# First token tiles and weights of a conditional mixture-of-LoRA layer: another order and other pieces on two DMA queues

## The chip, the cores and the metric

The kernel runs on one NeuronCore of a Trainium2 chip. The metric is the device time of one execution in microseconds (us). A core has TensorE (PE, matrix products into PSUM), VectorE (DVE), ScalarE (ACT), GpSimd (POOL) and SyncE (SP), each with its own instruction stream, and 16 DMA engines that all of them share. Here SyncE, ScalarE and GpSimd issue transfers. Engines wait for each other through semaphores.

## The reference

There are 8 sequences of 256 tokens with 1024 features in float32. Each sequence picks one of 8 weight matrices by its number. The result goes through a layer with a base matrix and a router that mixes two of eight rank-16 adapters, and is added to x:

```
w = weight[adapter_ids]
xc = jnp.einsum('bsi,boi->bso', x, w)
logits = xc @ W_router.T                       # softmax, top 2 of 8, renormalised -> combine
h = jnp.einsum('nd,erd->ner', xc, A_stack) * combine[..., None]
lora_out = jnp.einsum('ner,eor->no', h, B_stack) * 2.0
out = x + xc @ W_base.T + b_base + lora_out
```

## The kernel before

Every float32 operand of a product is split in two: a high part, which ScalarE makes with a cast, and a low part, which VectorE makes by subtracting the high one. The names are `x_hl` for tokens and `wc_hl` for weights. A product of high and low parts is then summed from several TensorE products of the fast float32 form.

The work runs in 2 groups of 4 sequences. For each sequence s, `cond` makes 8 output tiles t of the first einsum. A tile takes 8 steps k over the features: 8 wide products (line 801: high weights by high and low tokens, 512 columns) and then 8 narrow ones (line 805: low weights by high tokens, 256 columns). Router, adapters and the base matrix follow, the last in `second` with seven block products. Results leave through `out_sb`.

Raw float32 data comes in through `raw`, six slots of 512 KB (128 partitions of 4 KB). SyncE issues nearly all of these loads in one fixed order, `LOADS`, and before each waits until the slot's last user has been split (`wait_free`). A half of a sequence's tokens is one slot, ("x", s, half), with 4 of the 8 k. The weights of one output tile are one slot, ("w", s, t), with all 8 k. SyncE first reads the expert numbers from memory (line 362), because the address of a weight tile depends on them; it does so ahead of its first issue.

The first tiles are treated apart, by tables at lines 56 to 65. `START` gives the slots: X0 and X1 are the two token halves of sequence 0, W0 and W1 its first two weight tiles. `ACT_MOVES` and `SP_MOVES` list the pieces (tile, from k, to k) that ScalarE and SyncE issue, in order. A row of a piece is one partition's part of it. `HI_PIECES` and `LO_PIECES` list the pieces in which ScalarE casts (line 490) and VectorE subtracts (line 666), in order; each piece waits for the transfer or the cast that it needs. `START_STEPS` lists the steps (t, from k, to k) of `first_cond` on TensorE: all wide products of the step, then all its narrow ones. A wide product of step k waits for the high part of the weights at k and for the low part of the tokens at k; a narrow one waits for the low weights. From weights 2 on, ScalarE and VectorE take whole tiles (lines 472 and 536). Before its first real product TensorE does 26 products on zeroes (line 913).

Of the kernel before, what the change touches and what calls it, by code (L numbers as in the profile page):

```python
# [53 lines left out]


STARTS = 4
START = [("x", 0, 0), ("x", 0, 1), ("w", 0, 0), ("w", 0, 1), ("w", 0, 2), ("w", 0, 3)]
X0, X1, W0, W1 = range(STARTS)
ACT_MOVES = [(X0, 0, 4), (X1, 0, 4)]
SP_MOVES = [(W0, 0, 4), (W0, 4, 8), (W1, 0, 4), (W1, 4, 8)]  # L60
HI_PIECES = [(X0, 0, 2), (X0, 2, 4), (X1, 0, 2), (X1, 2, 4), (W0, 0, 2), (W0, 2, 4), (W0, 4, 8), (W1, 0, 4),
             (W1, 4, 8)]
LO_PIECES = [(X0, 0, 2), (X0, 2, 4), (X1, 0, 2), (X1, 2, 4), (W0, 0, 4), (W0, 4, 8), (W1, 0, 4), (W1, 4, 8)]

START_STEPS = [(0, 0, 8), (1, 0, 4), (1, 4, 8)]
WARM, WARM_N = 26, 2 * P

RESIDENT = {(0, 5): [("a", 0, 0)], (2, 5): [("b", 0, 0)]}
# [58 lines left out]
def split_order():  # L127

    order = START[STARTS:]
    for g in range(GROUPS):  # L130
# [23 lines left out]
def load_order():  # L154

    out, n = [], 0
    for g in range(GROUPS):
        ring = list(START) if g == 0 else []
        for s in range(GSEQS * g, GSEQS * (g + 1)):
# [19 lines left out]
def piece_count(pieces, i, k):  # L179

    return next(n + 1 for n, (j, a, b) in enumerate(pieces) if j == i and a <= k < b)


def tile_steps(i):
    return KT if START[i][0] == "w" else HT

# [19 lines left out]
def build(nc, x, ids, w_cond, w_base, w_router, lora_a, lora_b, bias, consts, out):  # L206
    with ExitStack() as ctx:
# [6 lines left out]
        def sem(name):  # L214
            return ctx.enter_context(nc.semaphore(name))
# [44 lines left out]
        raw_in = [sem(f"raw_in{i}") for i in range(RAW)]  # L260
        start_in = {(i, b): sem(f"start_in{i}_{b}") for i, a, b in ACT_MOVES + SP_MOVES if b < tile_steps(i)}
        warm_clear = sem("warm_clear")
# [49 lines left out]
        def split_dst(key, hl):  # L312
            kind, i, j = key
            if kind == "w":
                return wc_hl[:, slot_of(i, j), hl]
            if kind == "x":
                return x_hl[:, i % 2, HT * j:HT * (j + 1), hl, :]
            if kind == "S":
                return wc_hl[:, pair_of(i, j[0]) + j[1], hl]
            if kind == "T":  # L320
                return half(t_buffer(j[0]), j[1])[:, :, hl]
            if kind == "a":
                return a_hl[:, hl]
            return b_hl[:, hl, 0:KT] if kind == "b" else b_hl[:, hl, KT:]

        def split_src(key):
            kind, i, j = key
            if kind == "T":
                return half(t_plain(j[0]), j[1])
            if kind == "S":  # L330
                slot = S_FROM[j[0]] + j[1]
            else:
                slot = LANDED[("b", 0, 0) if kind == "bd" else key][0]
            v = raw[:, slot].rearrange("p (k n) -> p k n", n=TOK if kind == "x" else P)
            return v[:, 0:HT] if kind == "bd" else v

        def piece(v, i, a, b):

            n = v.shape[1] // tile_steps(i)
            return v[:, a * n:b * n]  # L340

        def piece_in(i, b):
            return raw_in[i] if b == tile_steps(i) else start_in[i, b]

        def move_piece(issuer, i, a, b, src):
            issuer.dma_start(piece(raw[:, i], i, a, b), piece(src, i, a, b)).then_inc(piece_in(i, b), 16)  # L346

        def moved(i, k):

            return piece_in(i, next(b for j, a, b in ACT_MOVES + SP_MOVES if j == i and a <= k < b))  # L350

        @block.sync
        def _(sp):
            ids_of = {}

            def source(key):
                kind, i, j = key
                if kind == "x":
                    return x[i, j]
                if kind == "w":  # L360
                    if i not in ids_of:
                        ids_of[i] = nc.sync.value_load(ids[0:1, i:i + 1], min_val=0, max_val=w_cond.shape[0] - 1)  # L362
                    return w_cond[bass.ds(ids_of[i], 1), j, :, :].rearrange("a p n -> (a p) n")
                if kind in ("a", "b"):
                    return lora_a if kind == "a" else lora_b
                oh, ih = next(q for name, _, q in QUARTERS if name == kind)
                return w_base[oh, ih, :, j, :]

            def wait_free(key):
# [6 lines left out]
                elif kind in ("A11", "A12", "A22", "A22b"):  # L376
                    j = {"A11": P7, "A12": P2, "A22": P3, "A22b": P4}[kind]
                    sp.wait_ge(lo_done, SPLIT["S", g, (j, h)])
                elif key in START[:STARTS]:
                    i = START.index(key)  # L380
                    sp.wait_ge(start_lo, piece_count(LO_PIECES, i, tile_steps(i) - 1))
                else:
                    sp.wait_ge(lo_done, SPLIT[("bd", 0, 0) if kind == "b" else key])

            in_slot = {}
            for i, a, b in SP_MOVES:
                move_piece(nc.sync, i, a, b, source(START[i]))
            for n, (key, slot) in enumerate(LOADS):
# [60 lines left out]
        def _(act):  # L449
# [35 lines left out]

            for i, a, b in ACT_MOVES:
                move_piece(nc.scalar, i, a, b, x[START[i][1], START[i][2]])
            for i, a, b in HI_PIECES:
                act.wait_ge(moved(i, b - 1), 16)
# [41 lines left out]
        def _(dve):  # L531
# [131 lines left out]

            for i, a, b in LO_PIECES:
                dve.wait_ge(start_hi, piece_count(HI_PIECES, i, b - 1))
                nc.vector.tensor_tensor(piece(split_dst(START[i], LO), i, a, b), piece(split_src(START[i]), i, a, b),
# [116 lines left out]
        def _(pe):  # L783
# [16 lines left out]
            def wide(ps, s, t, k):  # L800
                nc.tensor.matmul(ps[:], wc_hl[:, slot_of(s, t), HI, k], x_hl[:, s % 2, k].rearrange("p h n -> p (h n)"),  # L801
                                 start=(k == 0), stop=False)

            def narrow(ps, s, t, k):
                return nc.tensor.matmul(ps[:, TOK:], wc_hl[:, slot_of(s, t), LO, k], x_hl[:, s % 2, k, HI],  # L805
                                        start=False, stop=(k == KT - 1))

            def first_cond():

                for t, a, b in START_STEPS:  # L810
                    w, ps = (W0, W1)[t], bank_x[t]
                    for k in range(a, b):
                        pe.wait_ge(start_hi, piece_count(HI_PIECES, w, k))
                        pe.wait_ge(start_lo, piece_count(LO_PIECES, X0 if k < HT else X1, k % HT))
                        wide(ps, 0, t, k)
                    for k in range(a, b):
                        pe.wait_ge(start_lo, piece_count(LO_PIECES, w, k))
                        mm = narrow(ps, 0, t, k)
# [159 lines left out]
```

## Time and profile before

| | us |
|---|---|
| median of 3 runs | 396.82 |
| lowest and highest of them | 396.25, 397.05 |
| the profiled execution's own time | 396.74 |
| its span in the trace | 394.9 |
| TensorE busy in it | 389.9 (99%) |
| VectorE, ScalarE busy | 305.3, 183.7 |

The busy share tells how near an engine is to being the bound; the waits tell where it is not fed; the chain of work tells what released each step. DMA issues show in the rows of SPq and ACTq at the time of their issue, not of their transfer. Where a row of ScalarE says "idle before <-DMA", the transfer had landed at the row's start.

### The profile page before, as it was taken

The numbers are of one execution on the slowest core, as the hardware profiler recorded it, in microseconds if no ns is written. First come the engines' busy times: TensorE is split into PE (matmuls) and PEld (weight loads), VectorE is DVE, ScalarE is ACT, GpSimd is POOL, SyncE is SP. The second block draws the span as 40 slices with busy tenths as digits, with TensorE's granted clock in tenths as the row PEclk, the third lists the DMA queues.
The fourth block names the chain that finished last, engine by engine and source line by source line (L and its number), as shares of the span: only waits on it lengthen the run. The fifth ranks groups of instructions, "written<-read, shape, count | busy, mean of one in ns | idle before, by whom it ended". The sixth has DMA issues, their size and how long they took to land.

```text
span 394.9 us, 5677 instructions
## 1 busy us (share of the span) xinstructions
PE 389.9 (99%) x2174; PEld 332.1 (84%) x2174; DVE 305.3 (77%) x441; ACT 183.7 (47%) x282; POOL 40.1 (10%) x68
## 2 busy tenths in 40 slices
PE   8999999999999999999999999999999999999996
PEld 7888888888888888888888888888888888888885
DVE  4797967779699999984457786878867999999311
ACT  5777734748632434332146676356656224441000
POOL 0101100110000130021172000000000001301110
PEclk9999999999999999999999999999999999999999
DMA  7998782768430135586669877356073102462222
GB/s 259 391 341 310 282 299 80 272 217 309 146 106 0 54 115 173 192 289 218 218 222 369 337 240 240 108 168 244 15 266 122 41 1 80 162 185 80 82 80 80
DMA packets 21083, 72.96 MB, mean 185 GB/s; under 512 B 2816, under 2 KB 2832, under 8 KB 21056
## 3 DMA queue, kind: packets, MB, share of 16 engines
q1 hardware_dynamic: 15840, 55.58, 40.6%
q0 software_dynamic: 4928, 15.97, 11.3%
q10 hardware_dynamic: 288, 1.05, 0.7%
q8 instruction: 17, 0.28, 0.3%
q14 instruction: 10, 0.08, 0.1%
HBM read 64.20 MB, written 8.39 MB: 184 GB/s over the span
## 4 chain that ended last, share of the span: by engine, by line
PE 97%; DMA 1%; SPq 1%; DVE 0%; ACT 0%; issue 0%
PE bank_x L801 30%; PE bank_x L805 15%; PE bank_y L786 9%; PE bank_y L787 9%; PE bank_y L788 9%; PE bank_x L787 8%; PE bank_x L788 8%; PE bank_x L786 8%; PE bank_y L845 2%; DMA raw<-w_cond 1%; SPq L362 1%; PE bank_y L865 0%; DVE out_sb L587 0%; ACT wc_hl L490 0%; SPq L346 0%
## 5 line engine op out<-in xcount | busy, mean ns | idle before, releaser
L801 PE MATMUL bank_x<-x_hl,wc_hl 128*128 128x512 f32 x512 | 128.7, 392 | 0.6 <-ACT wc_hl L490 0.6
L536 DVE TENSOR_TENSOR wc_hl<-raw,wc_hl 128x1024 fp32r<-128x1024 f32 x90 | 108.4, 1221 | 19.0 <-ACT wc_hl L472 18.9
L472 ACT CAST wc_hl<-raw 128x1024 fp32r<-128x1024 f32 x90 | 93.4, 1050 | 55.6 <-DVE raw L540 23.1
L801 PEld LDWEIGHTS bank_x<-x_hl,wc_hl 128*128 128x128 f32 x512 | 92.2, 189 | 17.8 <-ACT wc_hl L490 1.2
L805 PEld LDWEIGHTS bank_x<-x_hl,wc_hl 128*128 128x128 f32 x512 | 70.0, 190 | 5.1
L805 PE MATMUL bank_x<-x_hl,wc_hl 128*128 128x256 f32 x512 | 71.5, 282 | 0.0
L424 POOL DMA_DIRECT2D out<-out_sb x28 | 15.3, 545 | 249.8 <-DVE out_sb L587 228.5
L504 ACT COPY xc_low<-bank_x 128x256 f32<-128x256 f32 x64 | 23.6, 369 | 32.6 <-PE bank_x L805 32.6
L786 PE MATMUL bank_x<-x_hl,wc_hl 128*128 128x512 f32 x96 | 37.3, 389 | 0.0
L787 PE MATMUL bank_x<-x_hl,wc_hl 128*128 128x512 f32 x96 | 37.3, 389 | 0.0
L788 PE MATMUL bank_x<-x_hl,wc_hl 128*128 128x512 f32 x96 | 37.3, 389 | 0.0
L687 DVE TENSOR_TENSOR xp<-bank_x,xc_low 128x256 f32<-128x256 f32 x64 | 26.9, 421 | 13.1 <-ACT xc_low L504 12.4
L509 ACT CAST xc_hl<-xp 128x256 fp32r<-128x256 f32 x64 | 26.0, 406 | 22.8 <-DVE xp L687 22.6
L579 DVE SCALAR_TENSOR_TENSOR out_sb<-bank_x,bias_sb,out_sb 128x512 f32<-128x512 f32 x32 | 23.6, 746 | 15.8 <-PE bank_x L788 15.1
L692 DVE TENSOR_TENSOR xc_hl<-xp,xc_hl 128x256 fp32r<-128x256 f32 x64 | 26.9, 420 | 7.5 <-ACT xc_hl L509 7.5
L587 DVE TENSOR_TENSOR out_sb<-bank_y,out_sb 128x512 f32<-128x512 f32 x24 | 16.4, 689 | 18.4 <-PE bank_y L788 17.6
L418 POOL DMA_DIRECT2D out_sb<-x x32 | 22.7, 714 | 73.9 <-PE bank_x L805 73.6
L786 PE MATMUL bank_y<-xc_hl,wc_hl 128*128 128x512 f32 x64 | 24.9, 389 | 0.0
L787 PE MATMUL bank_y<-xc_hl,wc_hl 128*128 128x512 f32 x64 | 24.9, 389 | 0.0
L788 PE MATMUL bank_y<-xc_hl,wc_hl 128*128 128x512 f32 x64 | 24.9, 389 | 0.0
L472 ACT CAST x_hl<-xp 128x1024 fp32r<-128x1024 f32 x16 | 16.6, 1052 | 15.1 <-DVE xp L540 14.7
L786 PEld LDWEIGHTS bank_x<-x_hl,wc_hl 128*128 128x128 f32 x96 | 18.0, 188 | 3.8
(91 smaller groups left out, 481.6 us busy)
## 6 DMA issues: line engine op xcount, KB each, us to landing
raw<-w_cond SPq DMA_DIRECT2D x62, 512.0 KB, 4.6
raw<-w_base SPq DMA_DIRECT2D x24, 512.0 KB, 5.2
out_sb<-x POOLq DMA_DIRECT2D x32, 256.0 KB, 5.1
raw<-x SPq DMA_DIRECT2D x14, 512.0 KB, 4.6
out<-out_sb POOLq DMA_DIRECT2D x28, 256.0 KB, 2.3
raw<-x ACTq DMA_DIRECT2D x2, 512.0 KB, 3.6
raw<-w_cond SPq DMA_DIRECT2D x4, 256.0 KB, 3.6
out<-out_sb SPq DMA_DIRECT2D x4, 256.0 KB, 2.0
```

Of the source, the lines that this page charges most:

```text
L472: nc.scalar.copy(split_dst(key, HI), split_src(key)).then_inc(hi_done, 1)
L504: nc.scalar.copy(xc_low[:, t % 2], bank_x[t % HT][:, TOK:]).then_inc(low_copied, 1)
L509: nc.scalar.copy(xc_hl[:, t, HI, s % 2 * TOK:(s % 2 + 1) * TOK], xp[:, s // 2 % 2, t, s % 2 * TOK:(s % 2 + 1) * TOK]).then_inc(xc_hi, 1)
L536: nc.vector.tensor_tensor(split_dst(key, LO), split_src(key), split_dst(key, HI).bitcast(F32), ALU.subtract).then_inc(lo_done, 1)
L579: nc.vector.scalar_tensor_tensor(out_sb[:, o], bank_x[m][:], bias_sb[:, i:i + 1], out_sb[:, o], ALU.add, ALU.add).then_inc(pass_done, 1)
L687: nc.vector.tensor_tensor(xc, bank_x[t % HT][:, 0:TOK], xc_low[:, t % 2], ALU.add) \
L692: nc.vector.tensor_tensor(xc_hl[:, t, LO, s % 2 * TOK:(s % 2 + 1) * TOK], xc, xc_hl[:, t, HI, s % 2 * TOK:(s % 2 + 1) * TOK].bitcast(F32), ...
L786: nc.tensor.matmul(ps, w_hi, v_hi, start=start, stop=False, skip_group_check=resumed)
L787: nc.tensor.matmul(ps, w_hi, v_lo, start=False, stop=False, skip_group_check=resumed)
L788: return nc.tensor.matmul(ps, w_lo, v_hi, start=False, stop=stop, skip_group_check=resumed)
L801: nc.tensor.matmul(ps[:], wc_hl[:, slot_of(s, t), HI, k], x_hl[:, s % 2, k].rearrange("p h n -> p (h n)"), start=(k == 0), stop=False)
L805: return nc.tensor.matmul(ps[:, TOK:], wc_hl[:, slot_of(s, t), LO, k], x_hl[:, s % 2, k, HI], start=False, stop=(k == KT - 1))
```

## The change

Only the tables of the start change. ScalarE's queue moves X0 alone, in two pieces of two k each, whose rows are 2 KB. X1 goes to SyncE's queue as one piece, behind the first half of W0 and ahead of its second half. ScalarE casts and VectorE subtracts in the new order of arrival, and the second half of W0 is cast in two pieces of two k. The first output tile is computed in two steps of four k, each with its wide and its narrow products, instead of one step of eight. The slots of X1 and W0 change places.

```diff
-START = [("x", 0, 0), ("x", 0, 1), ("w", 0, 0), ("w", 0, 1), ("w", 0, 2), ("w", 0, 3)]
-X0, X1, W0, W1 = range(STARTS)
-ACT_MOVES = [(X0, 0, 4), (X1, 0, 4)]
-SP_MOVES = [(W0, 0, 4), (W0, 4, 8), (W1, 0, 4), (W1, 4, 8)]
-HI_PIECES = [(X0, 0, 2), (X0, 2, 4), (X1, 0, 2), (X1, 2, 4), (W0, 0, 2), (W0, 2, 4), (W0, 4, 8), (W1, 0, 4),
-             (W1, 4, 8)]
-LO_PIECES = [(X0, 0, 2), (X0, 2, 4), (X1, 0, 2), (X1, 2, 4), (W0, 0, 4), (W0, 4, 8), (W1, 0, 4), (W1, 4, 8)]
-
-START_STEPS = [(0, 0, 8), (1, 0, 4), (1, 4, 8)]
+START = [("x", 0, 0), ("w", 0, 0), ("x", 0, 1), ("w", 0, 1), ("w", 0, 2), ("w", 0, 3)]
+X0, W0, X1, W1 = range(STARTS)
+ACT_MOVES = [(X0, 0, 2), (X0, 2, 4)]
+SP_MOVES = [(W0, 0, 4), (X1, 0, 4), (W0, 4, 8), (W1, 0, 4), (W1, 4, 8)]
+HI_PIECES = [(X0, 0, 2), (X0, 2, 4), (W0, 0, 2), (W0, 2, 4), (X1, 0, 2), (X1, 2, 4), (W0, 4, 6), (W0, 6, 8),
+             (W1, 0, 4), (W1, 4, 8)]
+LO_PIECES = [(X0, 0, 2), (X0, 2, 4), (W0, 0, 4), (X1, 0, 2), (X1, 2, 4), (W0, 4, 8), (W1, 0, 4), (W1, 4, 8)]
+
+START_STEPS = [(0, 0, 4), (0, 4, 8), (1, 0, 4), (1, 4, 8)]
```

What it moves on the engines. On SyncE, at the head of its stream, behind the reads of the expert numbers (the first weight piece, then the second):

```order
 L346 ISA
 L346 DMA raw<-w_cond 128x512
+L346 DMA raw<-x 128x1024
 L346 ISA
 L346 DMA raw<-w_cond 128x512
```

The transfer of X1 now stands between the two halves of W0; all that follows is the same, one transfer further back.

On ScalarE, from its transfers to the first whole weight tiles, before:

```order
1 L346 DMA raw<-x 128x1024 x2
2 L490 ACT_TABLE_LOAD
3 L490 CAST x_hl<-raw 128x2x256 x4
4 L490 CAST wc_hl<-raw 128x256 x2
5 L490 CAST wc_hl<-raw 128x512 x3
6 L472 CAST wc_hl<-raw 128x1024 x2
```

and after:

```order
1 L346 DMA raw<-x 128x512 x2
2 L490 ACT_TABLE_LOAD
3 L490 CAST x_hl<-raw 128x2x256 x2
4 L490 CAST wc_hl<-raw 128x256 x2
5 L490 CAST x_hl<-raw 128x2x256 x2
6 L490 CAST wc_hl<-raw 128x256 x2
7 L490 CAST wc_hl<-raw 128x512 x2
8 L472 CAST wc_hl<-raw 128x1024 x2
```

The two casts of X1 moved behind those of W0's first half, and W0's second half is two casts of two k.

On TensorE, from the warm-up to the third output tile, before:

```order
1 L913 MATMUL bank_y<-gate_rows 128x256 x26
2 L801 MATMUL bank_x<-x_hl,wc_hl 128x512 x8
3 L805 MATMUL bank_x<-x_hl,wc_hl 128x256 x8
4 L801 MATMUL bank_x<-x_hl,wc_hl 128x512 x4
5 L805 MATMUL bank_x<-x_hl,wc_hl 128x256 x4
6 L801 MATMUL bank_x<-x_hl,wc_hl 128x512 x4
```

and after:

```order
1 L913 MATMUL bank_y<-gate_rows 128x256 x26
2 L801 MATMUL bank_x<-x_hl,wc_hl 128x512 x4
3 L805 MATMUL bank_x<-x_hl,wc_hl 128x256 x4
4 L801 MATMUL bank_x<-x_hl,wc_hl 128x512 x4
5 L805 MATMUL bank_x<-x_hl,wc_hl 128x256 x4
6 L801 MATMUL bank_x<-x_hl,wc_hl 128x512 x4
```

Four narrow products of the first tile moved ahead of its last four wide ones.

## Rows read from the trace of the kernel before

**Rows 1.** The page's first part: busy time, share of the span, instructions.

```profile
PE 389.9 (99%) x2174; PEld 332.1 (84%) x2174; DVE 305.3 (77%) x441; ACT 183.7 (47%) x282; POOL 40.1 (10%) x68
```

**Rows 2.** TensorE's waits behind the warm-up: total us, times, longest.

```profile
PE bank_x L801 <- ACT wc_hl L490: 0.6, 2, 0.3
```

**Rows 3.** Chain of work, first 20 us: start us, us, what.

```profile
0.73 0.96 SPq L362
...
1.73 1.33 SPq L362
...
4.14 3.43 DMA raw<-w_cond
...
8.26 1.19 PE bank_x L801 x4
9.45 0.94 PE bank_x L805 x8
10.39 0.93 PE bank_x L801 x4
...
13.20 1.84 PE bank_x L801 x8
...
15.99 1.84 PE bank_x L801 x8
```

**Rows 4.** ScalarE in order of time: start us, us, operation, idle before it.

```profile
0.74 0.86 ACTq L346 DMA_DIRECT2D raw<-x  x2
...
4.01 2.36 ACT L490 CAST x_hl<-raw 128x512 fp32r<-128x512 f32 x4 [1.09 <-DMA raw<-x]
6.31 0.71 ACT L490 CAST wc_hl<-raw 128x256 fp32r<-128x256 f32 x2
7.59 0.62 ACT L490 CAST wc_hl<-raw 128x512 fp32r<-128x512 f32 x1 [0.56 <-DMA raw<-w_cond]
8.44 0.62 ACT L490 CAST wc_hl<-raw 128x512 fp32r<-128x512 f32 x1 [0.23 <-DMA raw<-w_cond]
10.43 0.62 ACT L490 CAST wc_hl<-raw 128x512 fp32r<-128x512 f32 x1 [1.38 <-DMA raw<-w_cond]
11.72 1.05 ACT L472 CAST wc_hl<-raw 128x1024 fp32r<-128x1024 f32 x1 [0.67 <-DMA raw<-w_cond]
13.02 1.06 ACT L472 CAST wc_hl<-raw 128x1024 fp32r<-128x1024 f32 x1 [0.25 <-DMA raw<-w_cond]
```

**Rows 5.** TensorE in order of time, from the warm-up to the first tile.

```profile
1.20 5.29 PE L913 MATMUL bank_y<-gate_rows 128*128 128x256 f32 x26 [1.20 <-DVE gate_rows L532]
...
6.77 1.19 PE L801 MATMUL bank_x<-x_hl,wc_hl 128*128 128x512 f32 x4 [0.29 <-ACT wc_hl L490]
8.26 1.19 PE L801 MATMUL bank_x<-x_hl,wc_hl 128*128 128x512 f32 x4 [0.30 <-ACT wc_hl L490]
```

**Rows 6.** SyncE's first issues in order of time.

```profile
3.56 2.00 SPq L346 DMA_DIRECT2D raw<-w_cond  x4
```

**Rows 7.** Stretches: busy us and instructions by engine, clock, DMA share, GB/s.

```profile
0.00:1.50 1.50, 0.30 (x1) 0.30 (x2) 0.27 (x1) 0.00 (x0) 0.40 (x5) 1.00 0.00 0
...
5.50:6.00 0.50, 0.50 (x6) 0.50 (x6) 0.50 (x2) 0.50 (x2) 0.00 (x0) 1.00 1.09 356
...
1.20:5.00 3.80, 3.80 (x18) 3.80 (x19) 0.34 (x1) 2.27 (x3) 0.00 (x0) 1.00 0.79 286
2.50:3.70 1.20, 1.20 (x7) 1.20 (x7) 0.00 (x0) 0.42 (x1) 0.00 (x0) 1.00 1.05 423
5.60:10.40 4.80, 4.21 (x25) 3.32 (x24) 3.55 (x6) 2.67 (x6) 0.00 (x0) 1.00 0.91 295
10.40:13.00 2.60, 2.60 (x16) 2.24 (x16) 0.89 (x2) 1.67 (x2) 0.00 (x0) 1.00 1.01 406
```

**Rows 8.** Groups of VectorE and ScalarE at the start: count, busy us, mean ns.

```profile
L666 DVE TENSOR_TENSOR x_hl<-raw,x_hl 128x512 fp32r<-128x512 f32 x4 | 2.5, 688 | 3.5 <-ACT x_hl L490 3.5
...
L490 ACT CAST wc_hl<-raw 128x256 fp32r<-128x256 f32 x2 | 0.7, 403 | 0.0
```

## The prediction

> **What bounds the kernel now.** I read the busy totals first: TensorE is busy 389.9 of 394.9 us [rows 1]. Then its waits: after its warm-up it waits twice, 0.6 us in all, both times for a ScalarE cast of weights [rows 2], and both waits lie before 8.3 us [rows 5]. From there to the last product nothing is late for TensorE, so whatever delays its stream in the first 15 us moves the end by the same amount, and whatever it saves there is at most those two gaps, 0.29 + 0.30 us. The third view is the chain of work at the start [rows 3]. The reader is to see in it that the chain goes over SyncE: 0.96 and 1.33 us of reading the expert numbers, then the issues, then 3.43 us until the second half of the first weights has landed, then a cast [rows 4] and the four 512-column products at 8.26. The fourth view is ScalarE's order of work [rows 4]: each cast there that stands behind an idle stretch ended by a DMA starts when that DMA has landed, so the view is a ladder of landings. In megabytes of SyncE's queue, which begins with nothing before it: the first 0.25 MB (first half of W0) by 6.31 at the latest (ScalarE was busy until then), 0.5 MB (second half of W0) 7.59, 0.75 MB (first half of W1) 8.44, 1.0 MB (second half of W1) 10.43, 1.5 MB (weights 2) 11.72, 2.0 MB (weights 3) 13.02. These rungs carry the forecast.
>
> **The first tokens on ScalarE's queue.** ScalarE issues at 0.74 [rows 4], while SyncE's first issue is at 3.56 [rows 6], behind the reads of the expert numbers. Before, ScalarE's two issues (1 MB) fill that time. Afterwards its queue holds only X0, 0.5 MB. X0 whole was castable at 4.01 [rows 4]; as two pieces the first should be castable about 0.6 us earlier (256 KB at the 423 GB/s of that stretch [rows 7]), the second at about 4.0 to 4.2, since rows of half the length may cost a little. Nothing on the path wants it: its last low half is done by 4.2 + 0.62 + 0.69 = 5.5 [rows 4, 8], and the first weights come at about 6. With X1 gone from this queue there is nothing for the 16 DMA engines to move from about 4.0 until SyncE's stream starts, one microsecond after its first issue (ScalarE's first issue at 0.74 had moved nothing by 1.5 [rows 4, 7]), so at about 4.6. The time is lost, not shifted.
>
> **The first half step.** W0's first half stays first on SyncE's queue. The casts of X1 no longer stand ahead of it on ScalarE (two of the four that ran to 6.37 [rows 4]), so its first cast may start at its landing. TensorE's warm-up runs to 6.49 and the first real product was at 6.77 [rows 5], so the gain here is between 0 and 0.28 us. TensorE then does four wide products and, new, the four narrow ones of the same k, and is through with them by about 8.1. That takes four narrow products, half of the 0.94 us of eight [rows 3], off what stands behind W0's second half. Neither gain is on the path by itself: the second half step waits for X1 and for W0's second half, wherever these are.
>
> **The second half step.** W0's second half was at 0.5 MB of SyncE's queue and is now at 1.0 MB, behind X1. Call its landing L. The cast of its first two k is 0.40 [rows 8] instead of 0.62, and a handover is about 0.04 (7.59 + 0.62 to 8.26), so TensorE goes on at L + 0.44. Then come four wide and four narrow products, 1.19 + 0.47 = 1.66. Before, this point was 8.26 + 1.19 + 0.94 = 10.39 [rows 3]. The shift of TensorE's stream is therefore L + 0.44 + 1.66 - 10.39 = **L - 8.29**. X1 is a second bound on the same start, because ScalarE casts it ahead of these k: it is at 0.75 MB, 8.44 by the ladder, ScalarE's two casts of it end 1.24 later at 9.68, and with 0.44 for W0's first two k the start is not before 10.12. Counted in starts, the shift is (start + 1.66 - 10.39), here +1.4.
> - Upper end of L: the rung as it stands, 10.43, a shift of +2.1. It contains the largest step of the ladder, 1.99 us for 256 KB, where the others are 0.65 to 1.28.
> - Evened out, the ladder goes from 6.31 to 13.02 in seven steps of 256 KB, 0.96 each, so L = 6.31 + 2.88 = 9.19, a shift of +0.9; X1 is then at 8.23, which by the bound above gives a start at 9.91 and +1.2.
> - Lower end: the stream at 406 GB/s from 4.6, as after 10.4 us [rows 7], not at the 295 of 5.6 to 10.4. Then X1 lands near 6.8, ScalarE's two casts end at 8.0, two k of W0 follow, TensorE goes on at 8.5: a shift of -0.2.
>
> **Behind it.** Every later piece also stands 0.5 MB further back. W1's first half, at 1.25 MB, lands at 11.07 by the ladder (half way from 10.43 to 11.72); with a cast of 0.62 it allows a start at 11.74 where before it was 10.39: a shift of at least 1.35. Evened out it is 10.15 and at least 0.4. Weights 2, at 2.0 MB, land at 13.02, are cast by 14.07, and the third product started at 13.20 [rows 3]: at least +0.9 in both readings. So the term that the landings of W0's second half give is backed by the two that follow it, and I take **+1.4 us**: the evened readings give 0.9 to 1.2, the rungs as they stand 1.35, 1.4 and 2.1, and only one of these asks for more. After weights 2 the stream brings a tile in 1.3 us and TensorE uses one in 2.79 (13.20 to 15.99), so nothing further is added. The load of weights 5 goes into the slot that now held W0, not X1, and its issue waits for W0's last low half, about 11 us; SyncE is held there, with weights 6 behind it. Its turn in the stream comes at about 15 and TensorE wants it at 13.20 + 3 x 2.79 = 21.6: cost nothing. VectorE and ScalarE do the same work plus one split cast (two of 0.40 for one of 0.62; its 0.18 is in the start that I reckon with).
>
> **Sum.** The profiled run was 396.74 us (span 394.9 and 1.8 around it), 0.08 under the median of 396.82. Plus 1.4 that is 398.1 against itself, and 398.2 against the median.
>
> **A rule against the trace.** The rows show SyncE's first issue 2.8 us after ScalarE's. The Trainium skill, page "DMA: Bandwidth & Descriptors", section "Issuing engines are not separate DMA queues", says that issuing from several engines only saves the sequencer's time to issue. By it the move of X1 would cost one issue, about 0.4 us, and the sum would be 397.2. The trace agrees that the engines are shared, but here one of the queues starts late, and that the rule leaves out.
>
> **Rivals.** (1) *The slow stretch is not one of bytes.* From 5.6 to 10.4 the engines moved 295 GB/s, after that 406 [rows 7]. If that was peculiar to the half-length weight pieces, and X1's full-length rows come at 406, X1 lands at 6.8 to 7.8, W0's second half at 7.6 to 9.1 and the shift is -0.2 to +0.8, in the middle +0.4: 397.2. For it: the x tiles moved at 423 on ScalarE's queue [rows 7]. Against it: the stretch also took in full-length weights. It decides where X1 lands before 7.8 and L is below 9.1. (2) *TensorE's clock falls in the new gap.* TensorE would now idle from about 8.1 to 9.6 or later, where its longest gap was 0.30. In the warm-up 18 products of 256 columns took 3.80 us [rows 7], 211 ns each, which is 1.2 GHz, where a narrow one later takes 0.94 / 8 = 118 ns; the slower pace held from 1.2 to about 5.5, where six such products take half a microsecond [rows 7]. The same again would cost 4.3 x (1 - 118 / 211) = 1.9 us on top: 400.1. For it: the gap is five times any other. Against it: TensorE has then worked for 7 us with few pauses. The page "TensorE: Matmul & The Clock Gate" of the Trainium skill (section "Part 1: The HAM clock gate") says that an idle engine falls back to half rate. The trace shows no fall after its two short gaps, and its column of the granted clock reads 1.00 even in the warm-up, so here it is the pace that tells. (3) *Faster.* The only time to win is the two gaps, 0.58 us, less than 0.2% of the whole; it needs L below 7.7.
>
> **How the numbers follow.** A measurement of this kernel can tell about 0.2%, 0.8 us, from no change. Forecast, slower without a fall of the clock: 0.60, itself 397.7 to 399.1. Rival 1, within 0.2%: 0.24. Rival 2, slower: 0.13. Faster by more than 0.2%, by something not named here: 0.03. So slower 0.73, same 0.24, faster 0.03. The range must leave out no more than two in ten: from 397.0 (most of rival 1) to 399.8 (L as late as 11.4, the ladder's rung and one step more), leaving rival 2 outside.
>
> **What would show it.** Right: ScalarE's first weight cast at or before 6.3; a wait of TensorE behind eight products, 1.4 to 2.7 us long, ended by a cast of W0 or by the low half of X1; the DMA share near zero between 4.0 and 4.6; the third product at 14.1 to 15.3 instead of 13.20; all later rows moved by the same amount. Wrong: the second half step starting before 9.3, a stretch from 4.6 to 8 at over 380 GB/s, products at 211 ns after the gap, or an end that moves by another amount than the third product does.

## The result and the profile after

The changed kernel takes 397.56 us (median of 22 runs, 396.89 to 399.77), the kernel before 396.70 (22 runs, 396.12 to 397.57). The ratio is 1.0024, 95% interval 1.0017 to 1.003: slower by 0.7 to 1.2 us, on the side and in the range that were forecast, and less than the +1.4 of the sum. It also lies just below the 397.7 to 399.1 that the prediction gave its main case. The profiled run took 397.39 us with a span of 395.6, against 396.74 and 394.9, so 0.7 us more.

ScalarE in order of time, the rows that answer to [rows 4] (start us, us, operation, idle before it and what ended it):

```profile
0.74 0.86 ACTq L346 DMA_DIRECT2D raw<-x  x2
...
3.42 1.22 ACT L490 CAST x_hl<-raw 128x512 fp32r<-128x512 f32 x2 [0.50 <-DMA raw<-x]
5.72 0.71 ACT L490 CAST wc_hl<-raw 128x256 fp32r<-128x256 f32 x2 [1.08 <-DMA raw<-w_cond]
7.73 1.14 ACT L490 CAST x_hl<-raw 128x512 fp32r<-128x512 f32 x2 [1.30 <-DMA raw<-x]
8.77 1.75 ACT L490 CAST wc_hl<-raw 128x256 fp32r<-128x256 f32 x4
11.34 1.05 ACT L472 CAST wc_hl<-raw 128x1024 fp32r<-128x1024 f32 x1 [0.81 <-DMA raw<-w_cond]
```

X1 was castable (landed, with ScalarE waiting for it) at 7.73; before, the casts of both x tiles were over by 6.37 [rows 4]. Behind it ScalarE does not wait again until 11.34: W0's second half was in before its casts began at 8.77. So of the two bounds that the prediction had for the second half step it was X1 with its casts, not W0's second half.

TensorE in the same view, which answers to [rows 5]:

```profile
1.20 5.16 PE L913 MATMUL bank_y<-gate_rows 128*128 128x256 f32 x26 [1.20 <-DVE gate_rows L532]
6.19 1.18 PE L801 MATMUL bank_x<-x_hl,wc_hl 128*128 128x512 f32 x4
7.21 0.74 PE L805 MATMUL bank_x<-x_hl,wc_hl 128*128 128x256 f32 x4
9.22 1.29 PE L801 MATMUL bank_x<-x_hl,wc_hl 128*128 128x512 f32 x4 [1.28 <-ACT wc_hl L490]
10.35 0.72 PE L805 MATMUL bank_x<-x_hl,wc_hl 128*128 128x256 f32 x4
```

The first half step starts at 6.19 instead of 6.77 and is done at 7.9. Then the new gap of 1.28 us opens. The chain of work, against [rows 3]:

```profile
1.60 0.66 SPq L362
...
3.20 4.51 DMA raw<-x
7.70 0.02 issue
7.73 1.14 ACT x_hl L490 x2
8.87 0.31 ACT wc_hl L490
9.18 0.04 issue
9.22 1.29 PE bank_x L801 x4
10.51 0.55 PE bank_x L805 x4
11.06 0.93 PE bank_x L801 x4
...
13.87 1.86 PE bank_x L801 x8
```

It goes over X1's transfer, 4.51 us from issue to landing, and no longer over W0's second half. The third tile's products start at 13.87 where it was 13.20. The second output tile starts at 11.06 where it was 10.39, so these 0.67 us are complete there, and they are the 0.7 by which the span grew: nothing was added or given back behind. The first row of this chain holds what the prediction did not have. The second of the two loads that read the expert numbers took 0.66 us, where it took 1.33 before [rows 3], and SyncE's first issue was at 2.76 instead of 3.56 [rows 6].

### The profile page after: what moved, and what is told of

Read it like the earlier page. It is cut to its first block, busy times and chain, and to the rows that moved or that the text cites. A ratio compares the mean times of both kernels' runs of the same rounds, so it can differ in the third digit from the quotient of the medians.

```text
span 395.6 us, 5679 instructions
## 1 busy us (share of the span) xinstructions
PE 389.9 (99%) x2174; PEld 331.9 (84%) x2174; DVE 305.5 (77%) x441; ACT 183.9 (46%) x283; POOL 40.1 (10%) x68
## 4 chain that ended last, share of the span: by engine, by line
PE 97%; DMA 1%; SPq 1%; ACT 0%; DVE 0%; issue 0%
PE bank_x L801 30%; PE bank_x L805 15%; PE bank_y L786 9%; PE bank_y L787 9%; PE bank_y L788 9%; PE bank_x L787 8%; PE bank_x L788 8%; PE bank_x L786 8%; PE bank_y L845 2%; DMA raw<-x 1%; SPq L362 0%; ACT x_hl L490 0%; PE bank_y L865 0%; DVE out_sb L587 0%; SPq L346 0%
## 5 line engine op out<-in xcount | busy, mean ns | idle before, releaser
L424 POOL DMA_DIRECT2D out<-out_sb x28 | 15.3, 545 | 249.8 <-DVE out_sb L587 228.5
```

## The experiments

Column two is the difference of the medians of the kernel and of the kernel before, run on the same chip; column three is the ratio that the comparison gave, with its interval; the two differ a little where the runs of a kernel spread. The last column counts the runs whose mean granted clock of TensorE was 0.996 or lower. Where only some runs of a kernel have it, these are its longest ones: with X0 in pieces and the steps alone, three runs took 397.80 to 398.22 us and three 399.72 to 400.26. There the median mixes two things, a late operand and a slower TensorE.

| kernel | us over before | ratio (95% interval) | clock 0.996 or lower |
|---|---|---|---|
| the change | +0.86 | 1.0024 (1.0017 to 1.003) | 1 of 22 |
| steps only | -0.13 | 0.9992 (0.9983 to 1.0001) | 0 of 12 |
| X1 back on ScalarE's queue | +0.78 | 1.0017 (1.0007 to 1.0027) | 1 of 12 |
| X1 alone moved | +4.40 | 1.0095 (1.0074 to 1.0115) | 4 of 4 |
| X1 alone moved, 52 warm-up products | +2.21 | 1.0059 (1.0046 to 1.0072) | 0 of 5 |
| X1 first on SyncE's queue | +1.13 | 1.0025 (1.0015 to 1.0035) | 2 of 11 |
| the change, X0 whole | +1.02 | 1.0026 (1.0016 to 1.0036) | 0 of 8 |
| the same, X1 back | +0.06 | 1.0001 (0.9993 to 1.001) | 0 of 11 |
| steps only, X0 in pieces | +2.12 | 1.0059 (1.004 to 1.0078) | 3 of 6 |
| the same, SyncE held | +0.72 | 1.0019 (1.001 to 1.0027) | 1 of 12 |
| the change, numbers not read | +2.45 | 1.0065 (1.0052 to 1.0078) | 3 of 5 |
| before, numbers not read | +3.49 | 1.009 (1.0077 to 1.0103) | 5 of 5 |
| steps only, W0 and W1 whole | +0.14 | 1.0006 (0.9998 to 1.0015) | 0 of 11 |

### First four: which part costs

Steps only:

```diff
 HI_PIECES = [(X0, 0, 2), (X0, 2, 4), (X1, 0, 2), (X1, 2, 4), (W0, 0, 2), (W0, 2, 4),
-             (W0, 4, 8), (W1, 0, 4), (W1, 4, 8)]
+             (W0, 4, 6), (W0, 6, 8), (W1, 0, 4), (W1, 4, 8)]
-START_STEPS = [(0, 0, 8), (1, 0, 4), (1, 4, 8)]
+START_STEPS = [(0, 0, 4), (0, 4, 8), (1, 0, 4), (1, 4, 8)]
```

> The kernel before with the other part of the change: both x tiles on ScalarE's queue as before, only the first output tile in two steps of four k and W0's second half cast in two pieces. Theory A: the four early narrow products fill the wait ahead of W0's second half; -0.2 to -0.45 us. Theory B: +0.3 to +0.9 us.

It measured -0.13 us, with an interval that just reaches no change. The steps are not what costs (this part of theory B falls here; the other part, W0 cast ahead of X1, is taken up by the last four runs). TensorE ran from 7.14 on without a pause, so the early narrow products do fill the second gap of [rows 5]. W0's first half landed at 6.68 in that profile, later than 6.31, which took part of the gain there; the interval, -0.7 to 0.0 us, does not tell the measurement from the -0.2 to -0.45 that were expected.

X1 back on ScalarE's queue:

```diff
-ACT_MOVES = [(X0, 0, 2), (X0, 2, 4)]
-SP_MOVES = [(W0, 0, 4), (X1, 0, 4), (W0, 4, 8), (W1, 0, 4), (W1, 4, 8)]
+ACT_MOVES = [(X0, 0, 2), (X0, 2, 4), (X1, 0, 4)]
+SP_MOVES = [(W0, 0, 4), (W0, 4, 8), (W1, 0, 4), (W1, 4, 8)]
```

> The changed kernel with X1 issued by ScalarE again, behind X0's two pieces; SyncE's queue is then W0, W0, W1, W1 as before, and all piece and step orders stay those of the change. Theory A (the cost is that X1's bytes are moved after SyncE's late start instead of before it, so W0's second half and all behind it come 0.5 MB later): X1 lands near 5, W0's second half near 7.6, the second half step starts at 8.3 to 8.8, and the time is -0.4 to +0.1 us against the kernel before. Theory B (the cost is in the new pieces and steps: more and smaller casts, W0 cast ahead of X1): it stays +0.5 to +0.9 us.

It measured +0.78 us. Theory A, as written, missed: putting X1 back gives almost nothing back, and the time is the one that theory B had expected. ScalarE's order shows another wait in its place, which theory B does not have:

```profile
4.75 0.62 ACT L490 CAST x_hl<-raw 128x512 fp32r<-128x512 f32 x1 [0.71 <-DMA raw<-x]
7.35 0.71 ACT L490 CAST wc_hl<-raw 128x256 fp32r<-128x256 f32 x2 [1.99 <-DMA raw<-w_cond]
7.97 1.14 ACT L490 CAST x_hl<-raw 128x512 fp32r<-128x512 f32 x2
```

SyncE issued W0's first half at 2.80, 0.76 us earlier than before, and yet it landed at 7.35 and not by 6.31. X0's last piece was castable at 4.75 and not at 4.0. From SyncE's start on both queues were moving at once.

X1 alone moved, casts and steps as before:

```diff
-ACT_MOVES = [(X0, 0, 4), (X1, 0, 4)]
-SP_MOVES = [(W0, 0, 4), (W0, 4, 8), (W1, 0, 4), (W1, 4, 8)]
+ACT_MOVES = [(X0, 0, 4)]
+SP_MOVES = [(W0, 0, 4), (X1, 0, 4), (W0, 4, 8), (W1, 0, 4), (W1, 4, 8)]
```

> The kernel before with one part of the change: X1 goes to SyncE's queue between W0's halves, while X0 stays one piece and the casts and steps keep the old order (X1 cast ahead of W0, one step of eight k). Theory A: all first products now wait for X1, near 7.7 to 8.4, and for two casts of it and one of W0, so TensorE starts at 9.4 to 10.1 with eight wide and eight narrow products ahead; +1.4 to +2.2 us against before, more than the whole change costs, because the half step does not hide any of it. Theory B: within 0.3 us of before.

It measured +4.4 us, twice what was expected. The first product came at 9.67, inside the 9.4 to 10.1 of theory A. The rest is mostly TensorE's pace. The first eight wide products, where 1.84 is usual [rows 3], and the stretches around them (the third number from the right is the granted clock):

```profile
9.67 3.78 PE L801 MATMUL bank_x<-x_hl,wc_hl 128*128 128x512 f32 x8 [3.26 <-ACT wc_hl L490]
```

```profile
6.40:9.60 3.20, 0.01 (x1) 0.00 (x0) 0.78 (x2) 1.43 (x4) 0.00 (x0) 0.88 0.97 321
9.60:13.40 3.80, 3.73 (x9) 2.97 (x10) 3.15 (x6) 2.96 (x7) 0.00 (x0) 0.50 1.02 403
13.40:16.00 2.60, 2.60 (x13) 2.42 (x12) 2.55 (x3) 1.82 (x3) 0.00 (x0) 0.57 1.01 400
```

The granted clock read 0.50, its level of 1.2 GHz, when work came again after a gap of 3.26 us, and it stayed there over the eight products.

X1 first on SyncE's queue, ahead of the read of the numbers:

```diff
-SP_MOVES = [(W0, 0, 4), (X1, 0, 4), (W0, 4, 8), (W1, 0, 4), (W1, 4, 8)]
+SP_MOVES = [(X1, 0, 4), (W0, 0, 4), (W0, 4, 8), (W1, 0, 4), (W1, 4, 8)]
```

> The changed kernel with X1 still on SyncE's queue but issued ahead of the reads of the expert numbers, at about 0.75. Theory A: X1 moves in the time that the change left empty and lands near 5; the reads of the numbers and so the weights start 0.4 us later; second half step at 8.6 to 9.2, 0.0 to +0.5 us against before, better than the change. Theory C (it is the queue: 0.5 MB more on SyncE's queue ahead of the weights costs the same wherever it is issued): +0.8 us or more.

It measured +1.13 us, outside what theory A gave and in the range of theory C. But it does not decide for theory C, since the weights started late. Both loads of the read became longer, in the view of line 362 (durations in ns, least, middle, greatest; start):

```profile
L362 SPq TENSOR_LOAD <-ids_ptr x1: 1540/1540/1540, 1.2 to 1.2; - x1
L362 SPq TENSOR_LOAD <-ids x1: 1517/1517/1517, 2.7 to 2.7; - x1
```

They took 0.96 and 1.33 us before [rows 3]. SyncE's first weight issue came at 4.75 instead of 3.56. Right behind the issue of X1 on its own queue the read of the numbers took longer. In the profiled run TensorE waited 2.02 us and its clock fell here too: four wide products took 2.08 us, at a granted clock of 0.50 from 8.00 to 10.10. That run is one of the two long ones of eleven (398.87 us); the other nine took 397.77 to 398.25 us at a mean clock of 0.999 or more, so the +1.13 us of the median holds no such fall.

### Second four: the rows of X0, the clock, the read

The change with X0 whole:

```diff
-ACT_MOVES = [(X0, 0, 2), (X0, 2, 4)]
+ACT_MOVES = [(X0, 0, 4)]
```

> The changed kernel with one part undone: X0 is one transfer of 4 KB rows again; all else stays changed. In five profiles so far SyncE's read of the expert numbers took 1.33 to 1.52 us beside whole x tiles and 0.66 to 0.67 beside X0's 2 KB pieces. Theory A2 (X1's place costs the forecast 1.4 us, and the shorter read gives 0.7 back): the read is at 1.3 to 1.5 again, SyncE's first issue at 3.5 to 3.6 instead of 2.8, and the time is +0.5 to +0.9 us above the changed kernel, +1.3 to +1.8 above before; the gap of TensorE grows and its pace may drop in some runs. Rival (the read's time is chance, or X0's pieces cost as much as they give): within 0.3 us of the changed kernel.

It measured +1.02 us against before, and by the ratios the same as the change (1.0026 and 1.0024). The first half of theory A2 held: the read's second load took 1.41 us and the first issue was at 3.53. The second half fell, and the rival (within 0.3 us of the changed kernel) held: the earlier issue in the changed kernel was worth little, since X1 landed at 7.93 here and at 7.73 there. DMA stretches of this run, the last number GB/s:

```profile
3.70:4.60 0.90, 0.90 (x6) 0.90 (x6) 0.00 (x0) 0.64 (x2) 0.00 (x0) 1.00 0.13 11
4.60:5.60 1.00, 1.00 (x6) 1.00 (x6) 0.99 (x2) 0.50 (x1) 0.00 (x0) 1.00 0.73 248
5.60:7.60 2.00, 1.86 (x12) 1.39 (x10) 0.95 (x2) 0.71 (x2) 0.00 (x0) 1.00 0.93 330
```

This is the empty stretch that the prediction named: 11 GB/s where the kernel before has 405 in the same 0.9 us.

Steps only, X0 in pieces:

```diff
-ACT_MOVES = [(X0, 0, 4), (X1, 0, 4)]
+ACT_MOVES = [(X0, 0, 2), (X0, 2, 4), (X1, 0, 4)]
```

> The steps-only kernel with X0 in two pieces of 2 KB rows, X1 behind it on ScalarE's queue; the casts keep the old order, X1 ahead of W0. It is the changed kernel with X1 back on ScalarE's queue and cast where it used to be. Theory A2 (the place of X1, with the cast order that goes with it, is what costs): first issue of SyncE at 2.8, X1 near 5.3, second half step at 8.4 or before; -0.5 to -0.1 us against before, so 1.0 to 1.4 us better than the change. Theory D (three issues and short rows on ScalarE's queue delay W0's first half to 7.35, as in the run with X1 put back): first product at 7.8, +0.1 to +0.6 us against before.

It measured +2.12 us, worse than either theory had it. Three of the six runs have the lower clock; the three without it took 397.93 us in the middle, +1.1, so about half of the median's loss goes with the clock, as far as the mean clocks tell; no trace of the three longer runs is at hand. The profiled run (397.93 us) is one without it. The read was short again (0.64 us) and SyncE issued at 2.76. X1, which everything waits for in this order of casts, was late:

```profile
6.84 1.14 ACT L490 CAST x_hl<-raw 128x512 fp32r<-128x512 f32 x2 [2.04 <-DMA raw<-x]
```

The chain in this profile is X1's transfer, 5.18 us from 1.64 on, and the first product came at 8.34. Weights that started 0.8 us earlier went through the same engines as X1. TensorE's gap was 1.71 us in this profile.

X1 alone moved, with 52 products on zeroes instead of 26:

```diff
-WARM, WARM_N = 26, 2 * P
+WARM, WARM_N = 52, 2 * P
```

> The kernel with X1 alone moved to SyncE's queue (measured at +4.4 us), with 52 products on zeroes instead of 26, which fill most of TensorE's gap of 3.26 us. If part of those 4.4 us is TensorE's slower pace after the gap (eight wide products took 3.78 us there, 1.84 elsewhere), the eight wide products take about 1.9 us and the time falls by 1.5 to 2.2 us, to +2.2 to +2.9 us against before. If all of it is the late arrival of X1, the time stays.

It measured +2.21 us, 2.2 us less for 26 more products that compute nothing, at the edge of what was expected. The granted clock reads 1.00 from 6.40 to 11.50, and the eight wide products took 1.92 us in the chain. The first real product came at 9.32 instead of 9.67, so up to 0.35 us of the gain may be a start that came earlier in that run. The clock's share of the +4.4 is then about 2 us, an estimate from these two kernels, and the rest is X1's late arrival.

The change without the read of the numbers for the first sequence:

```diff
+                if kind == "w" and i == 0:
+                    return w_cond[3, j]
                 if kind == "w":
                     if i not in ids_of:
```

> The changed kernel with the first sequence's weights taken at a fixed expert, 3, so that SyncE issues without the read of the numbers (the first sequence's result is then another; the numbers are read ahead of the second sequence's first weights). Theory A2 (late start of SyncE's queue is what makes X1's move dear): SyncE's first issue at 0.75, W0, X1 and W0's second half landed by about 6, no gap behind the first half step, real products from 6.2 without a pause: -1.3 to -0.9 us against before. Rival (X1 ahead of W0's second half costs wherever the queue starts, in casts and order): a wait of over 0.5 us stays behind the first half step.

It measured +2.45 us where theory A2 expected -1.3 to -0.9. Three of the five runs have the lower clock; the two without it, the profiled one among them, took 398.39 and 398.54 us, +1.5 and +1.7. SyncE issued at 0.76, 2.0 us earlier than in the change, and the kernel became slower. X0's second piece was castable at 7.51 instead of about 4.0, the first product came at 8.49. That refuted the idea behind my first theory, that the only harm lies in a queue's late start. The rival missed too: behind the first half step TensorE did not wait at all, since everything was late together.

### Last four: which bytes come first

The change with X0 whole and X1 back on ScalarE's queue:

```diff
-ACT_MOVES = [(X0, 0, 4)]
-SP_MOVES = [(W0, 0, 4), (X1, 0, 4), (W0, 4, 8), (W1, 0, 4), (W1, 4, 8)]
+ACT_MOVES = [(X0, 0, 4), (X1, 0, 4)]
+SP_MOVES = [(W0, 0, 4), (W0, 4, 8), (W1, 0, 4), (W1, 4, 8)]
```

> The changed kernel with X0 whole (measured at +1.0 us), and X1 behind it on ScalarE's queue, as one more part undone; casts and steps stay in the new order. The read of the numbers is then as long as before, and SyncE's stream starts when the x tiles are nearly in. Theory A (X1's move costs 1.0 to 1.4 us where SyncE's stream starts at the same time): X1 lands at 5.2, second half step at 8.6 to 8.9, -0.4 to +0.1 us against before. Theory D (the new order of casts costs, W0 ahead of X1): +0.5 us or more.

It measured +0.06 us, as theory A has it; that disposes of theory D here, and of what was left of theory B. Against the same kernel with X1 on SyncE's queue (+1.02) this is the clean price of X1's move where the queues start at the same times: 1.0 us, give or take 0.5 by the two intervals. The new order of casts costs nothing that could be seen; the second half step started at 8.58.

SyncE held until X0's first piece has landed, added to the kernel at +2.12:

```diff
-            for i, a, b in SP_MOVES:
-                move_piece(nc.sync, i, a, b, source(START[i]))
+            for n, (i, a, b) in enumerate(SP_MOVES):
+                src = source(START[i])
+                if n == 0:
+                    sp.wait_ge(start_in[X0, 2], 16)
+                move_piece(nc.sync, i, a, b, src)
```

> The kernel with X0 in pieces, X1 behind it on ScalarE's queue and the cast order of before (measured at +2.1 us), with one wait added: SyncE holds its first issue until X0's first piece has landed, about 3.4, instead of issuing at 2.76. Theory E (two queues in flight share the engines; weights that start early take the bandwidth from X1, which is wanted first): X1 lands near 5.3 instead of 6.8, and the time falls by 1.5 to 2.5 us, to -0.4 to +0.5 us against before, though a wait was added. Rival (X0's short rows or the third issue are slow by themselves): the time stays at +2 us or grows by the 0.7 us of the wait.

It measured +0.72 us: an added wait took 1.4 us off the median. SyncE now issued at 3.51 instead of 2.76, X1 was castable at 6.23 instead of 6.84, and the first real product came at 7.92 instead of 8.34. That accounts for 0.4 to 0.5 us, which is also what lies between the runs at full clock (397.43 against 397.93 us in the middle) and between the two profiled runs (397.43 and 397.93). The other 0.9 us of the medians go with the clock: one run of twelve has it lower, where three of six had. The direction is that of theory E, the size is less than it gave (1.5 to 2.5 us, X1 near 5.3), and what remains over the steps-only kernel is unexplained: the short rows, the third issue or the added wait cost something by themselves, which was not taken apart.

The kernel before without the read of the numbers:

```diff
+                if kind == "w" and i == 0:
+                    return w_cond[3, j]
                 if kind == "w":
                     if i not in ids_of:
```

> The kernel before with the first sequence's weights taken at a fixed expert, 3, so that SyncE issues at 0.75 beside ScalarE (the first sequence's result is another). Theory E: the weights' 1 MB and more share the engines with the x tiles from the start, X1 lands at 6.5 or later instead of 5.2, all casts of weights wait behind it, first product at 8 or later, +1 to +2.5 us against before. Rival (what counts is that the bytes start early): all operands are in by 6.5, real products from 6.5 on, -1.3 to -0.9 us.

It measured +3.49 us, past the upper end of theory E and 4.4 us away from the rival. ScalarE and TensorE:

```profile
5.47 1.14 ACT L492 CAST x_hl<-raw 128x512 fp32r<-128x512 f32 x2 [2.52 <-DMA raw<-x]
7.60 1.14 ACT L492 CAST x_hl<-raw 128x512 fp32r<-128x512 f32 x2 [0.98 <-DMA raw<-x]
```

```profile
9.10 3.78 PE L803 MATMUL bank_x<-x_hl,wc_hl 128*128 128x512 f32 x8 [3.00 <-ACT wc_hl L492]
```

The x tiles were castable at 5.47 and 7.60, 1.5 us and at least 2.4 us later than before (4.01, and the third of four casts in 2.36 us, so by 5.2, [rows 4]), though the engines moved more bytes from 4.6 on (414, 410 and 422 GB/s up to 9.6, against 268, 281 and 301). Up to 4.6 they had moved fewer, 348 GB/s from 2.5 to 3.3 against 415. Behind the gap of 3.00 us the granted clock was at 0.50, and all five runs have a mean clock of 0.995 or less. Taken from the pair with 26 and 52 warm-up products, that is about 2 of the 3.5 us, an estimate.

Steps only, with W0 and W1 each whole:

```diff
-SP_MOVES = [(W0, 0, 4), (W0, 4, 8), (W1, 0, 4), (W1, 4, 8)]
+SP_MOVES = [(W0, 0, 8), (W1, 0, 8)]
```

> The steps-only kernel with W0 and W1 each as one transfer of 4 KB rows instead of two of 2 KB. Rival 1 of the prediction asked whether the slow stretch (295 GB/s from 5.6 to 10.4) comes from the short rows of these pieces. If so, the stretch moves over 380 GB/s, W0 lands whole at about 7.2, W1 near 8.6, and the time is -0.5 to 0 us against before. If not, the rate stays near 300, W0's first half comes at 7.6 instead of 6.3 to 6.7, the first half step starts there, and the time is +0.3 to +1.0 us.

It measured +0.14 us. The rate came out as expected for the case that the short rows are slow, and the time did not follow it. The stretch from 5.6 to 7.6 of this kernel, and of the steps-only kernel behind it:

```profile
5.60:7.60 2.00, 0.66 (x7) 0.45 (x5) 1.73 (x3) 1.39 (x4) 0.00 (x0) 1.00 1.04 401
```

```profile
5.60:7.60 2.00, 0.69 (x4) 0.44 (x4) 1.88 (x4) 1.61 (x4) 0.00 (x0) 1.00 0.89 293
```

Whole rows moved 401 GB/s where the halves moved 293. Weights 2 were castable at 10.74 instead of 11.86. But the first half step now had to wait for all of W0, castable at 7.13 instead of 6.68, started at 7.59 instead of 7.14, and lost what the rate gave.

The rate is not the row length's alone, though. The kernel with X1 back on ScalarE's queue has W0 and W1 in halves like the kernel before. What the engines moved from 5.6 to 9.6 in the kernel before, and in that one:

```profile
DMA packets 534, 1.16 MB, mean 291 GB/s; under 512 B 59, under 2 KB 59, under 8 KB 534
```

```profile
DMA packets 670, 1.47 MB, mean 369 GB/s; under 512 B 74, under 2 KB 74, under 8 KB 670
```

The packets are equally short in the mean, 2.2 KB, and the second moved 369 GB/s with them; whole tiles moved 353 in those four microseconds. In the trace of the kernel before a 2 KB packet of this stretch took 84 ns (median) and a 4 KB one 159, so two short ones take 6% more than a long one, where whole tiles moved a third more than the 262 GB/s of the steps-only kernel. The rest are single packets that took longer and pauses, whose cause no run here shows; halving the number of transfers, which the whole tiles do as well, was not tried apart from the row length.

## Why the prediction was right, and where its sizes were off

**The bound and the direction** held. The start decides, the end moved by what the third tile moved (0.67 and 0.7 us), and the change is slower. The clean price of X1's move is 1.0 us (+1.02 against +0.06).

**Its own signs** did not come out so well. The first weight cast was before 6.3 (5.72), the gap was ended by a cast of W0, and all later rows moved alike. But the gap was 1.28 us and not 1.4 to 2.7, the third product came at 13.87 and not at 14.1 to 15.3, and the engines moved 300 GB/s from 4.0 to 4.6, where nothing should have moved. One sign of being wrong came true, a second half step before 9.3 (9.22); the others did not (304 GB/s from 4.6 to 8, no slow products in the profile). X1 at 7.73 and W0's second half by 8.77 are also the landings that the prediction reserved for rival 1, though the rate that rival 1 rests on did not show. So the time is right in side and range, while the main case was too slow throughout, and that the range reaches down to 397.0 is owed to rival 1.

**The empty stretch** was there, at another time: 70 GB/s from 3.30 to 3.80 in the changed kernel, and 11 GB/s from 3.70 to 4.60 with X0 whole.

**The first half step** gained more than its 0 to 0.28 us: it started at 6.19, not 6.77, right behind a warm-up that ended at 6.36. With SyncE starting as late as before (X0 whole) it started at 6.66, inside the forecast. As the prediction said, that gain is not on the path.

**The second half step** is where the size failed, and the term of the sum that was mis-sized is X1's landing. The rungs put X1 at 8.44 and the start at 10.12; measured were 7.73 and 9.22. Term by term, the forecast of +1.4 loses 0.71 us by X1's landing and 0.19 by what lies between it and the start (1.49 instead of 1.24 + 0.44), and gains 0.18 behind it: the four wide and four narrow products took 1.29 + 0.55 = 1.84 us instead of 1.66, because TensorE's weight loads waited 0.27 us for the second cast of W0's second half and 0.23 for its low half. That gives the 0.67 measured. The last two errors cancel, which is luck. In the kernel with X1 back and X0 whole this stretch took 1.26 + 0.55 us, so it comes with the new order of casts and not with X1's place.

Of the 0.71 us, 0.2 go with SyncE's earlier start: with X0 whole X1 landed at 7.93. The other 0.5 are the ladder. Its lowest rung, 6.31, was an upper bound, since ScalarE was busy until then, and W0's first half was castable at 6.20 there. From that on X1's 512 KB took 1.73 us, where the rungs gave 2.13 and the evened ladder 1.92. So the slow stretch was less slow for X1 than for the pieces from which the ladder was read. This touches rival 1, whose premise was that the slowness belongs to the half-length pieces. It is true in part at most: X1's stretch moved 330 GB/s with X0 whole and 309 in the changed kernel, not the 406 of the rival, and short packets moved 369 in the kernel with X1 back. What makes the stretch slow stays open.

**The lower end** of that landing was also reckoned too late: 0.79 MB at 406 GB/s from 4.6 on is X1 at 6.5, not 6.8. Nothing hangs on it.

**Behind it**, the bounds by W1 and weights 2 did not bind. Weights 2 were castable at 11.34, 1.7 us earlier than the 13.02 of the ladder, and at 11.92 with X0 whole.

**What was left out** is the read of the expert numbers. I took SyncE's first issue as fixed. The second load took 0.64 to 0.67 us in the four profiles with X0 in pieces and nothing ahead of the read on SyncE's queue, and 1.33 to 1.52 in the seven with X0 whole. Whether it is the length of the rows or their being two transfers, and why, was not tried. In the changed kernel the pieces and the earlier start together are worth about nothing, since the change with and without X0's pieces take the same time. With X1 on ScalarE's queue the same pieces and the same earlier start cost 0.7 us (+0.78 against +0.06) in the one order of casts and 1.2 in the other (+1.1 at full clock against -0.13; 2.2 by the medians). There the weights move beside both x tiles; that the sharing is part of it is shown by the run with SyncE held, how large a part is not.

**The rule weighed there**, that of the Trainium skill's page "DMA: Bandwidth & Descriptors", section "Issuing engines are not separate DMA queues", that issuing from several engines only saves issue time, gave 397.2 and the measurement is 397.56, with the clean price at 1.0 us where one issue is 0.4. What the rule also says, that the queues share the engines, turned out to matter more than I had used it for: in the kernel before without the read, where SyncE's queue starts 2.8 us earlier, both x tiles of ScalarE's queue are late.

**Rival 2**, the fall of the clock, did not happen in the profiled run, where the gap was 1.28 us. Among the 22 runs one took 399.77 us with a mean clock of 0.996, the lowest of them; no trace of it is at hand, so that it is this fall is an inference. The price of 1.9 us that the prediction gave is near the 2.2 us that the longer warm-up took off in the kernel with X1 alone moved, and near the 2 us between the two groups of runs of the steps-only kernel with X0 in pieces.

**No better version** came out of this. The steps alone are 0.08% faster with an interval up to 1.0001, which is not distinguishable from the kernel before.

## What to carry to other kernels

Read a start-up as one stream of bytes over shared DMA engines, ordered by what is wanted first, and not as queues that each should start as early as they can: here four of the five changes that started the weights earlier beside the x tiles made the kernel slower, and the fifth, X0's pieces in the changed kernel, made no difference. A ladder of landings from one profile gave the direction of the change, and X1 0.5 to 0.7 us too late. Where a change opens a gap on TensorE that was not there before, look at the granted clock of all runs before blaming the data: a median can mix runs at both levels, and one profile shows only one of them.

## What the runs showed of the hardware that I had not expected

- A read of a few numbers by SyncE goes with the transfers in flight: its second load took 0.64 to 0.67 us beside an x tile in two pieces of 2 KB rows, 1.33 to 1.52 beside one in 4 KB rows, and 1.52 behind a transfer of its own queue, where the first load took 1.54 instead of 0.84 to 0.96.
- Weights in whole tiles (4 KB rows) moved 401 GB/s where those in halves (2 KB rows) moved 293, in the same place of this start. Yet packets of 2 KB moved 369 GB/s in another order, and took 84 ns each where one of 4 KB took 159. The row length is thus not the whole of it.
- A queue started 2.8 us earlier made the other queue's second 0.5 MB tile land at least 2.4 us later, at a higher total rate from 4.6 us on and a lower one before.
- The granted clock stayed at 1.00 over gaps of TensorE of 1.28, 1.3 and 1.7 us in the profiled runs, and was at 0.50 behind gaps of 2.02, 3.00 and 3.26 us. The same kernel can do both: where the profile has the gap of 1.7 us three of six runs show a lower mean clock, and where it has the one of 2.02 us nine of eleven show none. With 26 more products on zeroes in the case of 3.26 us it stayed at 1.00 and the kernel was 2.2 us faster.
